# Projections of the next batch in another order over steps 9 to 15: logits ahead of k, the second group's q and k ahead of the V tiles, the ranks behind a V tile

## The chip, the cores and the metric

The kernel runs on one core of one Trainium2 chip. The metric is the device time of one execution in microseconds (us); lower is better. The engines are TensorE (PE; its weight loads are shown apart as PEld), VectorE (DVE), ScalarE (ACT), GpSimd (POOL) and SyncE (SP), whose queue starts most of the transfers.

## The reference

A layer over 8 batches of 512 tokens with 512 features: a layer norm, then attention with 16 heads and position bias, then a gate from a feed-forward block with two experts, of which each token uses the one with the larger logit.

```python
xn = layernorm(x)
qkv = xn @ Wqkv.T + b_qkv                       # 16 heads of 32
scores = q @ k.T * scale + alibi; causal mask
s = softmax(scores) @ v @ Wout.T + b_out
logits = xn @ w_router.T                         # 2 experts
top_idx = argmax(softmax(logits)); top_weight = its probability
h = xn @ w_fc[e].T; a = square(h if h >= 0 else h / 2)
g = silu(top_weight * (a @ w_proj[e].T))         # e = top_idx
out = x + s * g
```

## The kernel before

The program is written out by hand for each engine, without a scheduler; engines meet at counting semaphores (`wait(engine, semaphore, value)`). It has two stages, attention with the projections and the routing of the tokens, and behind it the feed-forward block, which works on tokens sorted by expert. The change touches the first.

Attention goes through the batches b = -1 to 8, each in 16 **steps**, one for each head. Iteration -1 is the start-up: it holds only the projections for batch 0. In a step TensorE turns the head's softmax weights (`ptrans`, line 446, in three parts into the banks psT0, psT1 and psT2), and computes the scores of the head four steps ahead (`scores`, line 425: four row groups of 128, 256, 384 and 512 columns in psS0, psS1 and psS2). Around and between them it does **jobs**. The list `JOBS` names each as (kind, batch relative to b, index), and `STEP` says which entries of the list belong to which step. The kinds are:

- `x`: turn 128 normalised tokens of the next batch (line 409).
- `q`, `k`: project one group of four heads, twelve matmuls of 512 columns (line 352, weights `wqkv` against `xT`). ScalarE copies the result out of PSUM (line 519), VectorE makes its high half (the **cast**, line 782), GpSimd its low half (line 947). SP's queue stores both to memory (line 280) and loads them back in the layout of the scores (line 285, function `stack`). Group 0 is read first by the scores of step 12 of the iteration before its own.
- `v`: the V tile of 128 tokens, twelve matmuls too; ScalarE copies it (line 544).
- `logits`: the router's logits, 48 matmuls of 2 columns; VectorE evaluates them (`choose`, lines 788 to 800).
- `rank`: two small matmuls (lines 400, 401) that count the tokens of each expert. VectorE turns them into positions (**place**, lines 807 to 823); GpSimd scatters the tokens' records with them in steps 14 and 15 (line 969).
- `ctx`: softmax weights times V of four heads (line 461), always the last work of its step. ScalarE copies it (line 528) at the beginning of the next step.
- `o`: the output projection.

Jobs use two PSUM banks in turn, psA0 and psA1: entry p of the list has the bank p mod 2, and `bank` lets it wait for the reader of the entry before in the same bank. So the order of `JOBS` sets the waits too. The other engines go through a step in a fixed order: VectorE takes a reciprocal for a head, masks and reduces the four score groups of the head three steps ahead (line 857), then does the reading for this step's jobs, then copies psT2 (line 844), and in some steps reduces a piece of the expert weights (line 888). GpSimd normalises the next head (line 941, four instructions), then makes q's or k's low half, and at steps 2, 7, 11 and 15 the context's (line 961). ScalarE copies psT0 and psT1 (line 566) and does the exponentials (line 579).

```python
            for p in STEP[step]:
                kind, db, i = JOBS[p]
                if job_exists(b, p) and kind in kinds:
                    yield kind, b + db, i, (odd + db) % 2, psA[p % ABANKS]
```

Of the kernel before, what the change touches and what calls it, by code (L numbers as in the profile page):

```python
# [95 lines left out]
def batches(eng, iteration):  # L96

    for b in range(-1, B + 1):
# [4 lines left out]
JOBS = [("q", 0, 2), ("ctx", -1, 3), ("k", 0, 2), ("q", 0, 3), ("k", 0, 3),  # L103
# [5 lines left out]
STEP = [(0, 1), (2,), (3,), (4,), (5, 6, 7), (8, 9), (10, 11), (12, 13),  # L109
        (14, 15), (16,), (17, 18), (19,), (20, 21), (22, 23), (24,), (25,)]  # L110
WMAX_AT = (5, 8, 12, 14)
WMAX_LAST = (2, 4, 9, 11)
ROUTE_AT = (1, 3, 5, 6)
# [1328 lines left out]
```

## Time and profile before

| what | value |
|---|---|
| median of 3 runs | 1499.54 us (1494.94 to 1501.87) |
| the profiled execution, whole | 1497.08 us |
| its span in the trace | 1495.3 us |
| mean granted TensorE clock | 0.984 of full |
| TensorE busy (matmuls) | 1392.0 us, 93% |
| VectorE busy | 929.4 us, 62% |
| ScalarE busy | 770.8 us, 52% |
| GpSimd busy | 684.8 us, 46% |

The attention stage fills a little more than the first half of the span, about 87 to 88 us for each batch. A busy share is a mean over stages; a busy TensorE is not one at its peak, since weights are loaded and instructions issued within it. The span leaves out what lies around it, here 1.8 us. In a row of the timeline stand the start, the length, the engine, the line, the operation and what is written and read; brackets give how long the engine was idle before, and who ended that.

### The profile page before, as it was taken

What the parts mean: (1) busy time and instruction counts of PE and PEld (TensorE: products, weight loads), DVE (VectorE), ACT (ScalarE), POOL (GpSimd) and SP (SyncE); (2) the same over time, 40 slices, a digit from 0 to 9 for tenths busy, and PEclk for the clock granted to TensorE, in tenths of its full rate; (3) what the DMA queues carried; (4) which work ended last, traced back from release to release, by engine and by line L of the source; (5) the groups of instructions that cost most, each with busy time, mean ns of one, the idle gap of its engine ahead of it and who ended that gap; (6) DMA issues with size and microseconds to landing.
All of it is one profiled execution on the core that took longest, in us unless ns stands there. A gap on an engine that the chain in (4) does not pass through costs nothing.

```text
span 1495.3 us, 30039 instructions
## 1 busy us (share of the span) xinstructions
PE 1392.0 (93%) x9863; PEld 883.6 (59%) x9863; DVE 929.4 (62%) x2441; ACT 770.8 (52%) x1824; POOL 684.8 (46%) x896
## 2 busy tenths in 40 slices
PE   2889999999999999999879999999999999999995
PEld 1455555655556565555546666666666666666663
DVE  7577776777767767777759855554445555544443
ACT  3477777777777777777736522222222222222221
POOL 0365656565575746556623433333333333333332
PEclk9999999999999999999999999999999999999998
DMA  4424424343342434334347411100111111001100
GB/s 159 142 85 133 136 93 142 113 129 107 117 146 92 149 99 136 107 111 148 106 141 229 139 44 44 43 29 24 35 43 41 39 43 44 24 27 38 36 29 29
DMA packets 84897, 133.45 MB, mean 89 GB/s; under 512 B 14095, under 2 KB 63247, under 8 KB 82576
## 3 DMA queue, kind: packets, MB, share of 16 engines
q1 hardware_dynamic: 75808, 105.70, 22.4%
q0 software_dynamic: 8944, 25.83, 5.5%
q8 instruction: 89, 1.46, 0.4%
q14 instruction: 56, 0.46, 0.1%
HBM read 97.81 MB, written 33.95 MB: 88 GB/s over the span
## 4 chain that ended last, share of the span: by engine, by line
PE 74%; DVE 11%; POOL 6%; issue 3%; ACT 3%; DMA 1%; DVEq 1%; SPq 0%; ACTq 0%; POOLq 0%
PE psF L1106 20%; PE psY L1126 19%; PE psA L352 18%; PE psT L446 7%; PE psA L461 5%; POOL pr L941 4%; PE psS L425 3%; DVE sg L1303 2%; PE psX L1080 1%; POOL route L969 1%; ACT stage L519 1%; PE psA L409 1%; DVE pr L857 1%; DVE stat L749 1%; DVE am L636 1%
## 5 line engine op out<-in xcount | busy, mean ns | idle before, releaser
L1106 PE MATMUL psF<-xT,wf 128*128 128x256 f16 (+1 forms) x3264 | 368.0, 269 | 0.0
L1126 PE MATMUL psY<-wf,aT 128*128 x1584 | 363.9, 379 | 0.4 <-DVE aT L1270 0.4
L1106 PEld LDWEIGHTS psF<-xT,wf 128*128 x3264 | 312.0, 98 | 63.5
L1344 POOL TENSOR_TENSOR a<-a 128x512 f32<-128x512 f32 (+1 forms) x136 | 153.3, 1127 | 391.0 <-DVE a L1261 389.4
L941 POOL TENSOR_SCALAR pr<-pr,rden 128x128 f32<-128x128 f32 (+3 forms) x512 | 269.7, 547 | 134.8 <-DVE rden L868 133.3
L579 ACT ACTIVATE pr<-pr,mn 128x128 f32<-128x128 f32 (+3 forms) x512 | 281.9, 553 | 0.0
L857 DVE CUSTOM_DVE_ANT_0 pr<-psS,base,nsl 128x128 f32<-128x128 f32 (+3 forms) x512 | 249.9, 543 | 2.4 <-PE psS L425 2.4
L1126 PEld LDWEIGHTS psY<-wf,aT 128*128 128x128 f16 x1584 | 154.5, 98 | 158.5 <-issue 1.1
L446 PE MATMUL psT<-conf,pr 128*128 128x128 f32 x1280 | 208.5, 282 | 21.2 <-POOL pr L941 17.2
L1183 ACT ACTIVATE rl<-psF 128x512 f32<-128x512 f32 (+1 forms) x136 | 79.3, 583 | 263.5 <-PE psF L1106 262.9
L446 PEld LDWEIGHTS psT<-conf,pr 128*128 128x128 f32 x1280 | 159.1, 144 | 87.3 <-POOL pr L941 27.1
L352 PE MATMUL psA<-xT,wqkv 128*128 128x512 f16 x768 | 195.2, 393 | 15.4 <-DVE wqkv L667 14.1
L1190 ACT ACTIVATE aT<-a 128x512 f16<-128x512 f32 (+1 forms) x136 | 84.0, 618 | 229.5 <-POOL a L1344 229.5
L1261 DVE SCALAR_TENSOR_TENSOR a<-psF,rl 128x512 f32<-128x512 f32 (+1 forms) x136 | 91.7, 674 | 169.3 <-ACT rl L1183 168.5
L566 ACT ACTIVATE pt<-psT 128x512 f32<-128x512 f32 x256 | 151.7, 593 | 80.6 <-PE psT L446 77.4
L1270 DVE TENSOR_TENSOR aT<-a,aT 128x512 f16<-128x512 f32 (+1 forms) x136 | 91.4, 672 | 129.0 <-ACT aT L1190 116.0
L352 PEld LDWEIGHTS psA<-xT,wqkv 128*128 128x128 f16 x768 | 76.7, 101 | 86.6 <-DVE wqkv L667 13.5
L947 POOL TENSOR_TENSOR pre<-stage,pre 128x512 f16<-128x512 f32 x64 | 74.3, 1161 | 110.1 <-DVE pre L782 110.1
L425 PE MATMUL psS<-ks,qs 128*128 128x128 f16 (+3 forms) x512 | 100.8, 304 | 22.7 <-DVE mn L857 18.9
L782 DVE CAST pre<-stage 128x512 f16<-128x512 f32 x64 | 33.7, 527 | 124.6 <-ACT stage L519 124.5
L352 PE MATMUL psA<-wout,cx 128*128 128x512 f16 x384 | 93.5, 386 | 7.3 <-POOL cx L961 7.3
L579 ACT ACTIVATION_READ_ACCUMULATOR pr<-pr,mn 128x1 f32 x512 | 98.3, 192 | 0.0
(155 smaller groups left out, 1371.5 us busy)
## 6 DMA issues: line engine op xcount, KB each, us to landing
qk_parts<-pre SPq DMA_DIRECT2D x64, 256.0 KB, 2.2
qs<-qk_parts SPq DMA_DIRECT2D x128, 128.0 KB, 2.7
ks<-qk_parts SPq DMA_DIRECT2D x128, 128.0 KB, 2.7
wst<-in_wf SPq DMA_DIRECT2D x16, 1024.0 KB
wstage<-in_wf SPq DMA_DIRECT2D x32, 512.0 KB, 5.0
xin<-in_x SPq DMA_DIRECT2D x32, 256.0 KB
attn_out<-so SPq DMA_DIRECT2D x32, 256.0 KB, 2.0
pt<-in_wqkv SPq DMA_DIRECT2D x4, 768.0 KB, 10.3
```

The lines of the kernel that those rows point to most:

```text
L352: last = nc.tensor.matmul(ps, a, x, start=(n == 0), stop=(n == len(pairs) - 1))
L425: nc.tensor.matmul(rows[i], qs[:, par, j, i * P:(i + 1) * P], ks[:, par, j, 0:(i + 1) * P], start=True, stop=True).then_inc(s["S_done"], 1)
L446: last = nc.tensor.transpose(ps[:, o:o + P], pr[:, j, c:c + P], conf[:, C_ID:C_ID + P])
L566: nc.scalar.activation(pt[:, g % 2, j, o:o + w], psT[r][:, 0:w], ACT.Copy).then_inc(s["T_act"], 1)
L579: nc.scalar.activation(p_, p_, ACT.Exp, bias=mn[:, c:c + 1], scale=-1.0, accum_out=den[:, c:c + 1]).then_inc(s["exp_done"], 1)
L857: nc.vector.tensor_tensor_reduce(out=pr[:, h % HG, ROWOFF[i]:ROWOFF[i] + w], in0=rows[i], in1=base[:, S - w:S], scale=nsl[:, h:h + 1], sca ...
L941: nc.gpsimd.tensor_scalar(p_, p_, rden[:, c:c + 1], 32768.0, ALU.mult, ALU.mult).then_inc(s["norm_done"], 1)
L1106: last = nc.tensor.matmul(psF[c % 2][:, k * TT:k * TT + tn], w(e, 2 * hc, hl, kc * 512 + col, P), xT[:, r % 2, x, kc, 0:tn], start=(m == 0 ...
L1126: last = nc.tensor.matmul(psY[r % 2][h][:], aT[:, c % 4, x, k, h * P:(h + 1) * P], w(e, 2 * hc + 1, hl, q * 512, 512), start=(c == 0 and k ...
L1261: nc.vector.scalar_tensor_tensor(out=part(a[:, c % 2, :], n), in0=part(psF[c % 2][:], n), scalar=2.0 ** -28, in1=part(rl[:, c % 2, :], n), ...
L1270: tt(aT[:, c % 4, 1, :, 0:tn], part(a[:, c % 2, :], n), aT[:, c % 4, 0, :, 0:tn], ALU.subtract).then_inc(s["U_lo"], 1)
L1344: nc.gpsimd.tensor_tensor(at, at, at, ALU.mult).then_inc(s["a_ready"], 1)
```

## The change

Two tables change, no function. The instructions stay the same in number and kind; their order over steps 9 to 13 and their banks change. In step 9 the logits come ahead of k of group 0, in steps 10 and 11 stand q and k of group 1, and V's four tiles follow in steps 12 to 15. In step 13 the V tile comes first and the rank behind it, though their places in the list are the other way round (`(23, 22)`), so V has psA1 and the rank psA0.

```diff
-        ("q", 1, 0), ("ctx", 0, 1), ("k", 1, 0), ("logits", 1, 0), ("v", 1, 0),
+        ("q", 1, 0), ("ctx", 0, 1), ("logits", 1, 0), ("k", 1, 0), ("q", 1, 1),
...
-        (14, 15), (16,), (17, 18), (19,), (20, 21), (22, 23), (24,), (25,)]
+        (14, 15), (16, 17), (18,), (19,), (20, 21), (23, 22), (24,), (25,)]
```

By steps this is:

| step | before | after |
|---|---|---|
| 8 | q0, ctx1 | q0, ctx1 |
| 9 | k0 | logits, k0 |
| 10 | logits, v0 | q1 |
| 11 | v1 | k1 |
| 12 | q1, ctx2 | v0, ctx2 |
| 13 | k1, rank | v1, rank |
| 14, 15 | v2; v3 | v2; v3 |

The first place is TensorE in step 13 of a middle batch, from the end of the context on. In brackets stands what an instruction waits for; `qk_staged` and `ctx_staged` are ScalarE's copies of a projection and of the context, `V_out` that of V. Before:

```order
L461 MATMUL psA1<-pt,v 32x128 x4
L446 MATMUL psT0<-conf,pr 128x128 [waits T_act,norm_done]
L446 MATMUL psT0<-conf,pr 128x128 x3
L352 MATMUL psA0<-xT,wqkv 128x512 [waits qk_staged]
L352 MATMUL psA0<-xT,wqkv 128x512 x5
L446 MATMUL psT1<-conf,pr 128x128 [waits T_act]
L446 MATMUL psT1<-conf,pr 128x128 x3
L352 MATMUL psA0<-xT,wqkv 128x512 x6
L400 MATMUL psA1<-e16,lt16 128x5 [waits e_ready,ctx_staged]
L401 MATMUL psA1<-epre,ones16 128x5
```

After, at the same place:

```order
L461 MATMUL psA1<-pt,v 32x128 x4
L446 MATMUL psT0<-conf,pr 128x128 [waits T_act,norm_done]
L446 MATMUL psT0<-conf,pr 128x128 x3
L352 MATMUL psA1<-wqkv,xT 128x512 [waits ctx_staged]
L352 MATMUL psA1<-wqkv,xT 128x512 x5
L446 MATMUL psT1<-conf,pr 128x128 [waits T_act]
L446 MATMUL psT1<-conf,pr 128x128 x3
L352 MATMUL psA1<-wqkv,xT 128x512 x6
L400 MATMUL psA0<-e16,lt16 128x5 [waits e_ready,V_out]
L401 MATMUL psA0<-epre,ones16 128x5
```

The wait for the context's copy has moved from the rank to the first matmul of the step's projection, which is now V's.

The second place is VectorE in step 13, from the last masked score group to the beginning of place (`rk` are the ranks, `R2_done` their matmuls). Before:

```order
L857 ISA pr,mn<-psS2,base,nsl 128x512 [waits S_done]
L857 ISA mn 128x1
L782 CAST pre<-stage 128x512 [waits k_stored,qk_staged]
L807 TENSOR_SCALAR rk<-psA1,esum 128x5 [waits meta_out,rexp_done,R2_done]
L810 COPY esum<-rk 128x1 [waits rank_read]
```

After:

```order
L857 ISA pr,mn<-psS2,base,nsl 128x512 [waits S_done]
L857 ISA mn 128x1
L807 TENSOR_SCALAR rk<-psA0,esum 128x5 [waits meta_out,rexp_done,R2_done]
L810 COPY esum<-rk 128x1 [waits rank_read]
L811 TENSOR_TENSOR t0<-tid,rk 128x4
```

The cast of k's second group, with its wait for ScalarE, has left the place ahead of the ranks; it stands in step 11 now.

The third place is TensorE in step 9 of a middle batch, behind the turning into psT0 (`wr` are the router's weights). Before, the twelve matmuls of k stood there alone. After:

```order
L446 MATMUL psT0<-conf,pr 128x128 x3
L352 MATMUL psA0<-wr,xT 128x2 [waits qk_staged]
L352 MATMUL psA0<-wr,xT 128x2 x41
L446 MATMUL psT1<-conf,pr 128x128 [waits T_act]
L446 MATMUL psT1<-conf,pr 128x128 x3
L352 MATMUL psA0<-wr,xT 128x2 x6
L352 MATMUL psA1<-xT,wqkv 128x512 [waits ctx_staged]
```

The logits' matmuls come from step 10; k follows them and has changed its bank. The order of SP's queue is the same, since it takes q and k group by group in either version.

## Rows read from the trace of the kernel before

**Rows 1.** The page's head and TensorE's row: busy time, share, instructions.

```profile
span 1495.3 us, 30039 instructions
...
PE 1392.0 (93%) x9863; PEld 883.6 (59%) x9863; DVE 929.4 (62%) x2441; ACT 770.8 (52%) x1824; POOL 684.8 (46%) x896
```

**Rows 2.** Waits over the whole span: total us, times, longest us.

```profile
PE psT L446 <- POOL pr L941: 17.2, 18, 1.9
```

**Rows 3.** Waits of TensorE from 403.3 to 410 us, same columns.

```profile
PE psS L425 <- DVE mn L857: 0.8, 3, 0.3
PE psT L446 <- DVE pt L844: 0.3, 1, 0.3
```

**Rows 4.** Timeline of TensorE, steps 12 to 0 of batch 3: start, length, line.

```profile
399.51 1.46 PE L352 MATMUL psA<-xT,wqkv 128*128 128x512 f16 x6
...
402.56 0.17 PE L401 MATMUL psA<-epre,ones 128*128 128x5 f16 x1
...
409.27 0.39 PE L425 MATMUL psS<-ks,qs 128*128 128x512 f16 x1 [0.33 <-DVE mn L857]
...
414.22 0.66 PE L446 MATMUL psT<-conf,pr 128*128 128x128 f32 x4 [0.20 <-POOL pr L941]
```

**Rows 5.** Timeline of ScalarE, step 13 of batch 3.

```profile
399.15 0.78 ACT L528 ACTIVATE cf<-psA,bqs,sc 128x512 f32<-128x512 f32 x1 [1.50 <-PE psA L461]
...
402.74 0.78 ACT L519 ACTIVATE stage<-psA,bqs,sc 128x512 f32<-128x512 f32 x1
```

**Rows 6.** Timeline of VectorE, steps 13 and 14 of batch 3.

```profile
403.55 0.43 DVE L782 CAST pre<-stage 128x512 f16<-128x512 f32 x1 [2.46 <-ACT stage L519]
...
403.89 0.22 DVE L807 TENSOR_SCALAR rk<-psA,esum 128x5 f32<-128x5 f32 x1
...
406.85 0.42 DVE L844 COPY pt<-psT 128x256 f32<-128x256 f32 x1
...
408.46 0.74 DVE L857 CUSTOM_DVE_ANT_0 pr<-psS,base,nsl 128x512 f32<-128x512 f32 x1
```

**Rows 7.** Timeline of TensorE: first instruction of steps 9, 10, 11.

```profile
378.43 0.66 PE L446 MATMUL psT<-conf,pr 128*128 128x128 f32 x4
...
382.72 0.60 PE L446 MATMUL psT<-conf,pr 128*128 128x128 f32 x4
...
388.18 0.60 PE L446 MATMUL psT<-conf,pr 128*128 128x128 f32 x4
```

**Rows 8.** Timeline of VectorE, steps 9 and 10 of batch 3.

```profile
382.97 0.43 DVE L782 CAST pre<-stage 128x512 f16<-128x512 f32 x1 [2.47 <-ACT stage L519]
...
385.68 0.22 DVE L788 TENSOR_SCALAR lg<-psA,sc 128x8 f32<-128x8 f32 x1
...
387.70 0.06 DVE L800 MEMSET t<- 128x1 f32 x1
```

**Rows 9.** Timeline of GpSimd, batch 3, behind step 9.

```profile
384.62 2.08 POOL L941 TENSOR_SCALAR pr<-pr,rden 128x128 f32<-128x128 f32 x4
```

**Rows 10.** Timeline of SP's DMA queue, batch 3: k's store behind step 9.

```profile
386.95 0.38 SPq L280 DMA_DIRECT2D qk_parts<-pre  x1
```

**Rows 11.** Timeline of the start-up: TensorE, ScalarE, VectorE.

```profile
58.16 0.17 PE L401 MATMUL psA<-epre,ones 128*128 128x5 f16 x1
...
59.26 2.75 PE L352 MATMUL psA<-wqkv,xT 128*128 128x512 f16 x12 [0.37 <-ACT stage L519]
...
58.33 0.78 ACT L519 ACTIVATE stage<-psA,bqs,sc 128x512 f32<-128x512 f32 x1 [7.40 <-PE psA L352]
...
59.48 0.22 DVE L807 TENSOR_SCALAR rk<-psA,esum 128x5 f32<-128x5 f32 x1
```

**Rows 12.** Waits of TensorE from 53 to 65 us, in the start-up.

```profile
PE psS L425 <- DVE mn L857: 1.8, 3, 1.2
```

**Rows 13.** Windows of two batches: length, busy by engine, mean clock, DMA.

```profile
168.35:255.12 86.77, 82.72 (x610) 49.22 (x610) 64.49 (x226) 66.48 (x181) 52.91 (x83) 1.00 0.39 123
255.12:343.60 88.48, 84.37 (x611) 50.09 (x611) 64.51 (x226) 66.48 (x181) 52.91 (x83) 0.98 0.39 120
```

2 rows, old and new, of the table JOBS are left out of this document.

## The prediction

> **What bounds the kernel now.** I read the page's head first. TensorE's matmul row is busy for 1392.0 of 1495.3 us [rows 1], so a microsecond is gained only where TensorE waits, and lost only where it is made to wait. The waits view says on whom: besides the start-up it waits on ScalarE, VectorE and GpSimd in short pieces, the longest of them 1.9 us, for GpSimd's normalisation of a head [rows 2]. The change touches steps 9 to 15 of a batch, so I laid the timelines of all engines over each other for one batch of the middle (b = 3, steps 9 to 15 from 378.4 to 418.6 us). From step 9 to the end of step 13 TensorE has no wait there at all. The waits stand behind it: in 403.3 to 410 us it waits 0.8 us for the row maxima and 0.3 us for a turned tile, both VectorE's [rows 3]. The same pieces stand at the same place in each of the seven batches b = 0 to 6, within 0.02 us. In the last batch there are no projections.
>
> What is late there can be followed back on VectorE [rows 6]. In step 13 the split of k's second group (the cast) starts at 403.55 us, since it waits for ScalarE's copy of k out of PSUM, 402.74 + 0.78 us [rows 5]. Only behind it comes the placing of the tokens (place): it starts at 403.89 and ends with the copy of psT2 at 406.85. Yet its own input, the rank, left TensorE at 402.56 + 0.17 = 402.73 us [rows 4]. So place, about 3 us of small dependent instructions, stands 1.1 us in a queue behind a cast that it doesn't need. All that follows on VectorE is late by it: the last masked row group at 408.46, and by it TensorE's last score matmul at 409.27 [rows 4, 6]. From there the lateness is carried on: GpSimd starts its normalisation late, sends its two scatters and normalises again, and TensorE's next step 0 starts at 414.22 with another 0.20 us of waiting for it [rows 4].
>
> **The change part by part.** The same instructions run, so all cost or gain is in waits.
>
> *Step 13, place first.* With k's second group in step 11, no cast stands before place. It can start when the rank is there. The first V product of step 13 pays for that: it now goes into the bank that the context of step 12 has just left, so it waits for ScalarE's copy of that context. This copy starts at 399.15 and takes 0.78, until 399.93 [rows 5]. How long TensorE takes to go on after such a copy is seen in the start-up: copy 58.33 + 0.78 = 59.11, matmul at 59.26, so 0.15 us [rows 11]. V would start at 400.08; the projection in its place starts at 399.51 now [rows 4]. That is a new wait of 0.57 us. The rank leaves 0.57 later, at 403.30; VectorE takes some 0.1 us to see it (my estimate, of the size of the 0.15 above), and place starts at 403.40 in place of 403.89: 0.49 us earlier. Because TensorE waits for VectorE in step 14 anyway, the 0.57 doesn't add to the end. By VectorE the last score matmul can come at 409.27 - 0.49 = 408.78. By its own work TensorE would have been there at 409.27 - 1.15 = 408.12 (1.15 is the sum of its waits, [rows 3] rounded), and now is there at 408.69. The later of the two holds: 408.78, with 0.1 us of waiting left of the 1.15. GpSimd's chain to 414.22 starts from the same VectorE instructions, so it moves by the same 0.49. Seven batches: 7 x 0.49 = 3.4 us. What queues behind the new wait is V's twelve matmuls, a transposition, the rank and the next scores, all of which have VectorE as their reader.
>
> The copy's length is worth a second look. The Trainium skill ("VectorE: DVE Perf Modes", section on the TRN2 errata) gives ScalarE reading PSUM 172 cycles plus one per element, at 1.2 GHz: (172 + 512) / 1.2 = 570 ns. The row has 0.78 us, with a bias and a scale from memory. By the page V would wait 0.21 us less and the sum would be 1.5 us larger; the measurement decides, and I stay with 0.78.
>
> *Start-up (b = -1).* The same queue, without a context ahead of V. The rank leaves at 58.16 + 0.17 = 58.33, place starts at 59.48 behind the cast [rows 11]. With 0.1 us to see it: 58.43, so 1.05 us earlier. TensorE then waits 1.8 us in three score matmuls for VectorE [rows 12], so the 1.05 goes through. The 0.37 us that V waits at 59.26 for k's copy goes too, but lies inside the same 1.05. Before that, k's first group comes behind the logits and its cast behind their evaluation; the scores wait for k's way through memory. That way goes through SP's queue, where q's loads stand ahead of k's store. I cost this at nothing, since in the start-up, too, the queue is what k's store waits for; the other bound is the evaluation's 2.0 us [rows 8], once, were the store to be late by all of it.
>
> *Steps 9 and 10, logits ahead of k.* The logits make step 10 last 388.18 - 382.72 = 5.46 us against 382.72 - 378.43 = 4.29 of step 9 [rows 7]. These 1.17 us move one step ahead; the sum of both is the same. On VectorE the evaluation takes 385.68 to 387.70 [rows 8]. In step 9 it can start once the logits are there, about 380.6 us by my estimate (378.43, two rounds of four transpositions and the 1.17), and ends near 382.6; k's cast, at 382.97 + 1.17 = 384.14 us [rows 8], waits for the copy of k anyway: evaluation costs nothing as long as VectorE idles there (it idles 2.47 us before that cast); without this cover it would be 2.0 us. k's store on SP's queue is at 386.95 behind q's loads [rows 10]. GpSimd ends k's low half at 384.62 in the trace [rows 9] and 1.17 later, at 385.79, in the new order, so the store stays where it is, and so do the scores that read it in step 12.
>
> *Steps 10 to 12, q and k of the second group, then V.* Each of these steps keeps its twelve matmuls of 512 columns. What is new is that three steps in a row (9, 10, 11) hand GpSimd a low half ahead of the next head's normalisation. In the trace the normalisation behind k's low half runs 384.62 to 386.70 [rows 9]. In the new order it ends 1.17 later, at 387.87; TensorE asks for it at 388.18 [rows 7]. The cover is 0.3 us. Cost nothing, bounds nothing and 0.2 us for each of three steps (4.2 us in seven batches). The stores and loads of this group move some 7 us ahead on SP's queue; in front of them stand k's loads of the first group, which they don't pass, and behind them x and the weights, which come earlier.
>
> *Sum.* -3.4 - 1.05 = -4.5 us. The profiled execution took 1497.08 us; it becomes 1492.6. The runs' median is 1499.54, 2.5 us above that execution, so I predict **1495.0 us**.
>
> **The rivals.** *The wait of V is hidden, or the clock falls less often.* If V finds its bank free, place starts 1.06 us earlier in each batch: 7 x 1.06 + 1.05 = 8.5 us, 1491.0. Against it speaks that the copy can't start before the context's last matmul. A batch in which TensorE's clock falls is 88.48 us at a mean of 0.98, one without is 86.77 at 1.00 [rows 13]: 1.71 us for each fall. Moving waits can take away two falls or add two (3.4 us either way). Chance of this rival 20%.
>
> *Nothing comes of it.* Place is earlier but GpSimd's row of normalisations in steps 10 to 12 passes its cover of 0.3 us: at 0.2 us beyond it, in three steps and seven batches, 4.2 us are given back. Time 1499 us. The thin margin speaks for it; against it, that the cover was worked out from rows that repeat to 0.02 us. Chance 17%.
>
> *Slower: the clock.* V's new wait of 0.57 us in step 13 and the 0.1 left in step 14 might bring TensorE from 2.4 to 1.2 GHz for a stretch in each batch. At 1.71 us a fall that is 12.0 us in seven batches, 7.5 slower in all: 1507 us. It decides from three falls on (5.1 against 4.5). Against it: step 14 waits 1.1 us today, more than the 0.7 us of both, and a batch that holds this wait still has a mean clock of 1.00 [rows 3, 13]; the fall in the other follows the long wait, up to 1.9 us, which the change leaves. Chance 8%. The Trainium skill ("TensorE: Matmul & The Clock Gate", section "What's actually happening") has the clock go down after an idle stretch and up after a busy one; by it alone no fall would be due, and 1495.0 would stand. The trace has falls after waits with matmuls between them, so the rule is no full cover.
>
> **How the numbers follow.** The forecast (3 to 6 us gained) has 55%, the rivals 20, 17 and 8%. A measurement of this kernel tells a change from none at about 0.5%, 7.5 us: the three runs of before lie 7 us apart. The first rival is faster than that; with some of the forecast's upper edge I give 25% to faster. The last rival is the 8% of slower, the rest, 67%, is the same. The range goes from the first rival with two falls fewer (1491.0 - 3.4, rounded to 1487.5) to no gain with one or two falls more (1499.5 + 2.5 = 1502); it leaves out the last rival and some of the edges.
>
> **What would show it.** Right: in the middle batches the place instructions start behind the masked rows with VectorE idle before them, waiting for TensorE's rank; a wait of 0.4 to 0.7 us of TensorE on ScalarE's context copy at the start of step 13, seven times; the score waits of step 14 shorter, about 0.1 in place of 1.15 us; a batch without a fall 86.3 us. Wrong: TensorE waits on GpSimd in steps 10 to 12; place still begins behind something else; more stretches at 1.2 GHz than before.

## The result: 1.3% faster, outside the predicted range

| | before | after |
|---|---|---|
| median | 1500.70 us (4 runs, 1494.94 to 1502.18) | 1480.60 us (4 runs, 1477.33 to 1481.51) |
| profiled execution; its span | 1497.08; 1495.3 us | 1481.51; 1479.7 us |
| mean granted TensorE clock | 0.984 | 0.987 |

The ratio is 0.9874 (95% interval 0.9857 to 0.9891): 20.1 us less by the medians, 15.6 us by the two profiled executions, where 4.5 were forecast. The timeline of TensorE in the same batch as [rows 4, 7], steps 10 to 0:

```profile
377.08 0.60 PE L446 MATMUL psT<-conf,pr 128*128 128x128 f32 x4
...
392.36 0.66 PE L446 MATMUL psT<-conf,pr 128*128 128x128 f32 x4
393.32 1.47 PE L352 MATMUL psA<-wqkv,xT 128*128 128x512 f16 x6 [0.31 <-ACT cf L528]
...
396.39 0.17 PE L401 MATMUL psA<-epre,ones 128*128 128x5 f16 x1
...
397.21 0.60 PE L446 MATMUL psT<-conf,pr 128*128 128x128 f32 x4
...
399.38 1.46 PE L352 MATMUL psA<-wqkv,xT 128*128 128x512 f16 x6
400.68 0.38 PE L446 MATMUL psT<-conf,pr 128*128 128x128 f32 x2
400.89 0.71 PE L425 MATMUL psS<-ks,qs 128*128 128x128 f16 x4
401.44 0.63 PE L446 MATMUL psT<-conf,pr 128*128 128x128 f32 x4
...
406.04 0.66 PE L446 MATMUL psT<-conf,pr 128*128 128x128 f32 x4 [0.19 <-POOL pr L941]
```

The step starts stand at 392.36 (13), 397.21 (14) and 401.44 (15). Step 14 now holds no wait at all. VectorE in steps 13 and 14, to be laid beside [rows 6]:

```profile
396.61 0.23 DVE L807 TENSOR_SCALAR rk<-psA,esum 128x5 f32<-128x5 f32 x1 [3.14 <-PE psA L401]
...
396.94 0.15 DVE L811 TENSOR_TENSOR t<-tid,rk 128x4 f32<-128x4 f32 x1
...
398.71 0.42 DVE L844 COPY pt<-psT 128x256 f32<-128x256 f32 x1
...
400.31 0.75 DVE L857 CUSTOM_DVE_ANT_0 pr<-psS,base,nsl 128x512 f32<-128x512 f32 x1
```

Place begins behind 3.14 us of idle time, 0.05 after the rank's end (396.39 + 0.17), and takes 2.10 us to the copy of psT2; it took 2.96 in [rows 6]. The 0.86 between them is one instruction. These are rows of the kernel before that the prediction had not looked at, from the timelines of VectorE, GpSimd and TensorE:

```profile
404.21 1.02 DVE L811 TENSOR_TENSOR t<-tid,rk 128x4 f32<-128x4 f32 x1
...
404.06 1.16 POOL L947 TENSOR_TENSOR pre<-stage,pre 128x512 f16<-128x512 f32 x1 [2.72 <-DVE pre L782]
...
399.02 0.65 PE L446 MATMUL psT<-conf,pr 128*128 128x128 f32 x4
...
403.38 0.60 PE L446 MATMUL psT<-conf,pr 128*128 128x128 f32 x4
...
405.55 1.46 PE L352 MATMUL psA<-wqkv,xT 128*128 128x512 f16 x6
407.33 0.44 PE L446 MATMUL psT<-conf,pr 128*128 128x128 f32 x2 [0.32 <-DVE pt L844]
408.06 0.34 PE L425 MATMUL psS<-ks,qs 128*128 128x128 f16 x2 [0.30 <-DVE mn L857]
408.60 0.34 PE L425 MATMUL psS<-ks,qs 128*128 128x384 f16 x1 [0.20 <-DVE mn L857]
...
409.57 0.66 PE L446 MATMUL psT<-conf,pr 128*128 128x128 f32 x4
```

L811, the third instruction of place, subtracts two operands of four columns in SBUF. It ended at 404.21 + 1.02 = 405.23, and GpSimd's low half of k, which started 0.15 us ahead of it and ran beside it, at 404.06 + 1.16 = 405.22. All eight instances in the trace of before take 1019 to 1027 ns, all eight after 150 to 153 ns, with no low half beside them. Step lengths of TensorE, from such starts, in us:

| step | 9 | 10 | 11 | 12 | 13 | 14 | 15 | sum |
|---|---|---|---|---|---|---|---|---|
| before | 4.29 | 5.46 | 4.23 | 6.61 | 4.36 | 6.19 | 4.65 | 35.79 |
| after | 5.52 | 4.23 | 4.22 | 6.83 | 4.85 | 4.23 | 4.61 | 34.49 |

The logits' 1.2 us moved from step 10 to 9 at no cost. Step 12 is 0.22 longer: VectorE's high half of the context (L900), 0.42 us in most instances, takes 1.28 there, again beside GpSimd's low half of k, which now falls on it. The seven kernels of this study with such a cast of 1.27 to 1.28 us have a step 12 of 6.81 to 6.83 us, the other five one of 6.61; no run takes the collision away alone, so this cause is argued and not shown.

```profile
386.29 1.16 POOL L947 TENSOR_TENSOR pre<-stage,pre 128x512 f16<-128x512 f32 x1 [1.04 <-DVE pre L782]
...
386.46 1.28 DVE L900 CAST cx<-cf 128x512 f16<-128x512 f32 x1
```

Steps 13 and 14 together fell from 10.55 to 9.08 us, by 1.47. The whole batch, in the windows view (columns as in [rows 13]):

```profile
391.56:477.02 85.46, 82.21 (x614) 49.27 (x610) 63.95 (x226) 66.44 (x181) 52.70 (x82) 1.00 0.41 127
```

It is 85.46 us against 86.77 without a fall of the clock. Between the first and the last full batch's place, before needs 527.49 us for six batches, four of them with a fall (88.46), after 512.80 without any: 6 x 1.31 + 4 x 1.71 = 14.7 us. That is nearly the whole 15.6; the part ahead of it is level and the part behind it gives 0.9.

### The profile page after: what moved, and what is told of

The parts are those of the page before. It is cut to its first block, busy times and chain, and to the rows that moved or that the text cites. A ratio compares the mean times of both kernels' runs of the same rounds, so it can differ in the third digit from the quotient of the medians.

```text
span 1479.7 us, 30039 instructions
## 1 busy us (share of the span) xinstructions
PE 1384.0 (94%) x9863; PEld 880.8 (60%) x9863; DVE 923.9 (62%) x2441; ACT 770.7 (52%) x1824; POOL 682.5 (46%) x896
## 4 chain that ended last, share of the span: by engine, by line
PE 75%; DVE 10%; POOL 6%; ACT 3%; issue 3%; DMA 1%; DVEq 1%; SPq 0%; ACTq 0%; POOLq 0%
PE psY L1126 19%; PE psF L1106 19%; PE psA L352 19%; PE psT L446 7%; PE psA L461 5%; POOL pr L941 4%; PE psS L425 3%; DVE sg L1303 2%; PE psX L1080 1%; POOL route L969 1%; PE psA L409 1%; DVE stat L749 1%; DVE am L636 1%; ACT stage L519 1%; DVE wf L1225 1%
## 5 line engine op out<-in xcount | busy, mean ns | idle before, releaser
L352 PE MATMUL psA<-xT,wqkv 128*128 128x512 f16 x768 | 188.8, 386 | 14.4 <-DVE wqkv L667 13.1
```

The costliest lines, as they stand in the source:

```text
L352: last = nc.tensor.matmul(ps, a, x, start=(n == 0), stop=(n == len(pairs) - 1))
```

## The experiments

The medians are of 4 to 11 executions each, on chips on which the kernel before had medians of 1499.88 (first four), 1499.73 (next four) and 1501.02 us (last two). The ratio is that to the kernel before on the same chip; the whole change has 0.9874, so variants whose intervals overlap with 0.9857 to 0.9891 aren't told apart from it by their time. "Falls" counts those of TensorE's clock in the six batches just named, in the one execution of each that has a trace.

| run | median us | ratio (95%) | batch without a fall | falls in 6 |
|---|---|---|---|---|
| rank_first | 1480.23 | 0.9869 (0.9851 to 0.9887) | 84.65 | 2 |
| low_late | 1500.51 | 1.0006 (0.9997 to 1.0015) | 86.65 | 4 |
| lock_back | 1494.21 | 0.9961 (0.9948 to 0.9975) | 86.42 | 3 |
| logits_first | 1500.27 | 1.0004 (0.9995 to 1.0013) | 86.80 | 5 |
| pad3 | 1488.37 | 0.9927 (0.9911 to 0.9943) | 86.12 | 2 |
| pad6 | 1498.45 | 0.9991 (0.9981 to 1.0001) | 86.76 | 5 |
| v_bank | 1478.04 | 0.9850 (0.9834 to 0.9866) | 84.98 | 2 |
| rank_first_after | 1478.28 | 0.9856 (0.9838 to 0.9874) | 84.50 | 3 |
| rstd_late | 1496.57 | 0.9973 (0.9963 to 0.9983) | 86.93 | 5 |
| rstd_late_vbank | 1480.04 | 0.9866 (0.9851 to 0.9881) | 85.17 | 0 |

**Only step 13 (rank_first).** The kernel before, with the rank ahead of k's product; the transpositions into psT1, which stand between the halves of a product, move ahead of the rank (`mid()`).

```diff
-        (14, 15), (16,), (17, 18), (19,), (20, 21), (22, 23), (24,), (25,)]
+        (14, 15), (16,), (17, 18), (19,), (20, 21), (23, 22), (24,), (25,)]
...
                 ps = bank(b, p)
+                mid()
                 wait(pe, s["e_ready"], batch + 1)
```

> The kernel before with one pair of numbers changed: in step 13 the rank comes ahead of k's second group (with psT1's transpositions ahead of both), nothing else is moved. Theory 1 (step 13 alone: place stands behind the cast, and its first two-operand instruction, 1.02 us in the trace of before against 0.15 after, is held by GpSimd's low half beside it): place starts right behind the masked rows, is over before the cast, L811 takes 0.15 us, step 14 falls from 6.19 to about 4.23 us, a batch without a fall of the clock from 86.77 to about 84.8, so at least 13 us less than before (7 x 1.9), more if falls of the clock go away. Theory 2 (the gain comes from moving q and k ahead of V in steps 10 to 12): no gain beyond the 0.6 us that I had worked out for place, under 5 us.

Measured: 1480.23 us, as good as the whole change. Its timeline of VectorE (lines one higher):

```profile
390.65 0.22 DVE L808 TENSOR_SCALAR rk<-psA,esum 128x5 f32<-128x5 f32 x1
...
390.98 0.15 DVE L812 TENSOR_TENSOR t<-tid,rk 128x4 f32<-128x4 f32 x1
...
393.30 0.43 DVE L783 CAST pre<-stage 128x512 f16<-128x512 f32 x1 [0.47 <-ACT stage L520]
```

Place stands ahead of the cast, so ahead of the low half that follows it, and its L812 is short. Steps 13 and 14 last 4.39 and 4.22 us. A batch is 0.81 us shorter than in after: V has no new wait (0.48), step 12 no collision (0.22), and step 15 is 0.16 shorter. So everything that the change gains in a batch can be had from the order of place and cast; moving V, q, k and the logits isn't needed for it.

**Only the low half away (low_late).** The kernel before; in step 13 GpSimd makes k's low half only when place has ended.

```diff
                     w = int(kind == "k")
+                    if step == 13:
+                        wait(pool, s["meta_ready"], nxt + 1, s["apart_pool"])
```

> The kernel before, but GpSimd makes k's low half of step 13 only when place is over; the order of the jobs stays, and place stays behind the cast. Theory 1 (GpSimd's low half holds VectorE's two-operand instruction): L811 falls from 1.02 to 0.15 us, place is 0.87 us shorter, step 14 falls from 6.19 to about 5.3 us, 6 us less in seven batches. Rival (L811 is long for a reason of its own, as waiting for its input): L811 stays at 1.02 us and the time as before.

Measured: no change, where 6 us had been expected. L811 fell to 0.15 us although place still stood behind the cast, so the low half was what held it. But the low half now stands in front of the normalisation on GpSimd's queue, and TensorE waits for that instead at the start of step 15; step 14 is 6.07 us, not the 5.3 expected:

```profile
405.97 1.16 POOL L949 TENSOR_TENSOR pre<-stage,pre 128x512 f16<-128x512 f32 x1 [4.89 <-DVE rk L823]
407.11 2.05 POOL L941 TENSOR_SCALAR pr<-pr,rden 128x128 f32<-128x128 f32 x4
...
409.22 0.66 PE L446 MATMUL psT<-conf,pr 128*128 128x128 f32 x4 [0.67 <-POOL pr L941]
```

**The neighbour put back (lock_back).** The kernel after, with an added GpSimd subtraction of the low half's size on two constant tiles, released by the rank. Its result is not used.

```diff
+                if more and step == 13:
+                    wait(pool, s["R2_done"], nxt + 1, s["apart_pool"])
+                    nc.gpsimd.tensor_tensor(scrap[:], bout[:], base[:], ALU.subtract)
```

> The changed kernel with one extra GpSimd instruction per batch in step 13: a subtraction of 128x512 between two constant tiles into a scratch tile, started when the rank is there, so beside place. Theory 1: L811 is about 1.0 us again in place of 0.15; the last masked rows come 0.87 us later, of which TensorE feels about 0.75 after a slack of 0.1, so 5 us more than the changed kernel in seven batches, about 1486 us, if the clock falls as it does there. Rival (L811's length has nothing to do with GpSimd): 0.15 us and 1480.6.

Measured: 1494.21 us, 13.6 of the 20 us given back, where 5 had been expected.

```profile
403.83 1.01 DVE L812 TENSOR_TENSOR t<-tid,rk 128x4 f32<-128x4 f32 x1
...
403.55 1.27 POOL L952 TENSOR_TENSOR scrap<-bout,base 128x512 f16<-128x512 f32 x1 [2.95 <-PE psA L402]
```

The two end together again (404.84 and 404.82), though no semaphore ties them and no tile is common. A batch is 0.96 us longer; steps 13 and 14 are 4.85 + 5.08 = 9.93 us. This splits the 1.47: from 10.55 to 9.93 the earlier start of place, 0.62; from 9.93 to 9.08 the end of this collision, 0.85. The rest of the 13.6 is falls: 7 x 0.96 = 6.7, and four falls more (three in the six batches, one behind them), 6.8.

**Only the logits (logits_first).** The kernel before with the logits ahead of k, and nothing else.

```diff
-        ("q", 1, 0), ("ctx", 0, 1), ("k", 1, 0), ("logits", 1, 0), ("v", 1, 0),
+        ("q", 1, 0), ("ctx", 0, 1), ("logits", 1, 0), ("k", 1, 0), ("v", 1, 0),
...
-        (14, 15), (16,), (17, 18), (19,), (20, 21), (22, 23), (24,), (25,)]
+        (14, 15), (16, 17), (18,), (19,), (20, 21), (22, 23), (24,), (25,)]
```

> The kernel before with the first part of the change alone: logits ahead of k in step 9, the V tile alone in step 10; steps 11 to 15 as before. Theory 1: no effect, 1500 us within 3, steps 9 and 10 only exchange 1.2 us. Theory 2 (part of the gain comes from here, as the evaluation of the logits leaves step 10, where GpSimd normalises beside it): some us less, L792 falls from 0.51 to 0.16 us, and a batch is shorter by some tenths.

Measured: no change, 86.80 us a batch. In the start-up it isn't free: the first scores start at 54.15 us, in before at 53.32. k's store goes out 0.26 us later, and its loads 3.4 us behind the store and not 2.9. Why the loads come later isn't shown; in the traces with the logits first they follow the store by anything from 2.2 to 3.8 us.

**The same work, longer (pad3, pad6).** The kernel after, with 3 or 6 further matmuls of 512 columns in each batch, ahead of the logits, whose results are overwritten. They ask whether the missing falls hang on the order or on the batch's length. Here with 6:

```diff
                 ps = bank(b, p)
+                for t in range(6):
+                    nc.tensor.matmul(ps[:], wqkv[:, 0, 0, 0:P], xT[:, par, 0, 0, :], start=True, stop=True)
```

> As the kernel with six more matmuls per batch, but three: 0.65 us more per batch, 86.1 us. Theory 1: 1480.6 + 4.5 and some falls of the clock (1 to 4), 1487 to 1492 us. Rival (no falls by length): 1485.1 us.

> The changed kernel with six more matmuls of 512 columns per batch ahead of the logits (their results are overwritten), 6 x 0.216 = 1.3 us of TensorE work, which makes a batch as long as it was before the change: 86.8 us. Theory 1 (the falls of TensorE's clock behind the wait of step 3 come with how the batches lie in time, not with the order of the jobs): 3 to 5 falls in batches 1 to 6 where the changed kernel's trace has none, time 1480.6 + 9.1 + 4 x 1.7 = 1496.5 us. Rival (the change took the falls away itself, with step 14's waits): no falls there, 1480.6 + 9.1 = 1489.7 us.

Measured: 1.30 us more in each batch (pad6) is 9.1 us, and the time rose by 17.9; 0.66 (pad3) is 4.6, and it rose by 7.8. The difference is 8.8 and 3.2 us, and 5 and 2 falls at 1.71 are 8.6 and 3.4. Two windows of pad6, a batch with a fall and one without:

```profile
404.64:493.07 88.43, 85.15 (x618) 50.70 (x616) 63.96 (x227) 66.55 (x182) 52.72 (x82) 0.98 0.38 119
493.07:579.83 86.76, 83.51 (x618) 49.89 (x616) 63.94 (x226) 66.53 (x182) 52.72 (x82) 1.00 0.39 122
```

With the new order and the old length the falls are back, as the theory of both runs had it. So the new order of jobs doesn't by itself keep them away.

**V's wait (v_bank, rank_first_after).** The kernel after; v_bank exchanges V and rank in the list and keeps V first, so V no longer waits for the context's copy. rank_first_after puts the rank first, as in rank_first.

```diff
-        ("k", 1, 1), ("v", 1, 0), ("ctx", 0, 2), ("rank", 1, 0), ("v", 1, 1),
+        ("k", 1, 1), ("v", 1, 0), ("ctx", 0, 2), ("v", 1, 1), ("rank", 1, 0),
...
-        (14, 15), (16, 17), (18,), (19,), (20, 21), (23, 22), (24,), (25,)]
+        (14, 15), (16, 17), (18,), (19,), (20, 21), (22, 23), (24,), (25,)]
```

> The changed kernel with the V tile and the rank of step 13 exchanged in the list of jobs, so that they change banks; their order in the step stays. V no longer waits for ScalarE's copy of the context. Theory 1: the wait of 0.31 us (0.47 from start to start) at the head of step 13 goes, a batch 85.0 us in place of 85.46, 3.3 us less in seven batches if the clock falls as in the changed kernel. Rival (VectorE bounds step 14 again, as place isn't earlier by the same): no gain.

> The changed kernel with the rank ahead of the V tile in step 13, behind the transpositions into psT1. Theory 1: place starts behind the masked rows, V's wait for the context's copy is hidden by the transpositions; a batch 84.9 us against 85.46, 4 us less in seven batches. Against the kernel of before with the rank first (84.65 us) it is 0.2 us longer per batch, since the context's high half in step 11 meets GpSimd's low half of k (L900, 1.28 us) and step 12 is longer by 0.2. Rival (moving q and k has a gain of its own): shorter than 84.65 us.

Measured: step 13 is 4.37 us in v_bank, 0.48 less than in after, step 14 stays 4.22. The wait was in full on TensorE's path: 7 x 0.48 = 3.4 us, and two falls take the same back: the profiled spans are 1478.7 and 1479.7 us. The medians, 1478.04 and 1478.28, are the lowest of the study; their ranges overlap with that of after.

rank_first_after had been expected at 84.9 us a batch and is at 84.50, 0.15 under rank_first. There its rival held, that moving q and k has a gain of its own. Step 12 is 0.21 longer than in rank_first, but step 15 is 4.23 us against 4.45, with no wait for GpSimd at its end. By the timelines this takes both parts: no low half stands ahead of GpSimd's normalisation, as one does in rank_first, and place is over early, as it isn't in after (4.61). In time the two aren't told apart (1480.23 and 1478.28 us).

**The long wait moved (rstd_late, rstd_late_vbank).** GpSimd's inverse deviations of the layer norm (L953, L956) move from step 1 to step 2, behind the normalisation, and their use on VectorE from steps 2 to 5 to steps 3 to 6; once in before and once in v_bank.

```diff
-                    elif step < 6:
-                        ln_apply(step - 2)
+                    elif 3 <= step < 7:
+                        ln_apply(step - 3)
...
-                if more and step == 1:
+                if more and step == 2:
```

> The kernel before, with GpSimd's inverse deviations of the layer norm (veps and rstd, in step 1, ahead of the normalisation) moved to step 2 behind the normalisation, and the layer norm's application moved from steps 2 to 5 to steps 3 to 6. TensorE's wait for that normalisation is 1.80 us, and the inverse deviations wait 0.79 us for VectorE and take about 1.4 with what lies between. Theory (the falls of the clock hang on this wait): the wait shrinks to some 0.4 us, a batch is about 1.4 us shorter (85.3 without a fall) and no batch of 1 to 6 has a fall: 1499.7 - 9.8 - 6.8 = about 1483. Rival (falls come whatever the wait, as the batches lie in time): still 2 to 5 falls, about 1490. Rival on the other side: rstd now ends some 3 us later than today, the lows behind it too, and VectorE or SP's transfers wait for them: no shorter batch, about 1500.

> The same move of the inverse deviations and of the layer norm's application, on top of the changed kernel with V and rank exchanged in the list (1478.0 us, 2 falls in the middle batches, 84.98 us a batch). Theory: 83.6 us a batch without a fall and no fall: 1478.0 - 9.8 - 3.4 = about 1465, faster than both kernels. Rival: falls stay, about 1468. Other side: later lows are waited for, about 1478.

Measured: the move didn't do what it was made for. The wait of 1.80 us is only passed on, as one of 1.9, since GpSimd works without a pause through step 2 and the next normalisation ends late. So neither the shorter batch came (some 1483 and 1465 us had been expected), nor was the theory tested that the falls go when this wait goes. From rstd_late, GpSimd and TensorE:

```profile
428.36 1.04 POOL L950 TENSOR_TENSOR rstd<-veps,half 128x4 f32<-128x4 f32 x1
429.39 1.15 POOL L956 TENSOR_TENSOR pre<-stage,pre 128x512 f16<-128x512 f32 x1
430.51 1.15 POOL L961 TENSOR_TENSOR cx<-cf,cx 128x512 f16<-128x512 f32 x1
431.76 2.55 POOL L941 TENSOR_SCALAR pr<-pr,rden 128x128 f32<-128x128 f32 x4
...
434.36 0.66 PE L446 MATMUL psT<-conf,pr 128*128 128x128 f32 x4 [1.92 <-POOL pr L941]
```

A batch is 0.16 us longer than in before, and 0.19 longer than in v_bank. The profiled execution is level with that of before (1497.15 and 1497.08); where the medians' 4.4 us come from isn't settled. With the same wait of 1.9 us one kernel has 5 falls in six batches and the other none, so the wait alone doesn't decide.

## Why the prediction was wrong

**The term that was mis-sized** is that of "Step 13, place first": 7 x 0.49 = 3.4 us. Steps 13 and 14 measured 7 x 1.47 = 10.3, of which step 12 gave 7 x 0.22 = 1.5 back; with 0.06 in the other steps a whole batch is 1.31 us shorter, 9.2 in seven. The direction and the first link of the mechanism, place behind a cast that it doesn't need, were right. Three things made the term too small.

*Place's length.* The prediction carried "place, about 3 us of small dependent instructions" along at its old length. Inside stood L811 with 1.02 us beside neighbours of its kind at 0.16. low_late and lock_back show that GpSimd's low half was its cause, and lock_back what it costs: 0.85 us a batch, more than the whole forecast of 0.49. A look at each row of place, and at what GpSimd did in that microsecond, would have found it.

*The ceiling.* "By its own work TensorE would have been there at 409.27 - 1.15" summed the idle times in brackets. With it, no more than 1.15 us could have come out of step 14; 1.96 did (6.19 to 4.23). The matmuls' ends are modelled and overlap the next one's start: without a stall the turning of a tile starts 1.30 us behind the group of six matmuls ahead of it (399.38 to 400.68), with one 1.78 (405.55 to 407.33). That is 0.48 us lost where the bracket says 0.32. From the turning to the next step it is 0.76 without and 2.24 with waits, 1.48 lost, of which the brackets name 0.83. V's wait shows the same: 0.47 by the starts (393.32 - 392.36, against 0.49 without), 0.31 in brackets.

*The start of place.* It is 0.62 us earlier, not 0.49: V's wait is 0.47 and not 0.57, since TensorE goes on 0.05 us behind the copy (392.49 + 0.78, then 393.32) and not 0.15, and VectorE sees the rank after 0.05 and not 0.1. But "the 0.57 doesn't add to the end" held only under the lower gain. With the collision gone step 14 has no wait left to hide it, and v_bank shows its 0.48 in full.

**Steps 10 to 12** were costed at nothing, with GpSimd's cover of 0.3 us as the risk. The cover held: no wait of TensorE there. The cost came from elsewhere: 0.22 us in step 12, by all signs from the same kind of collision.

**Steps 9 and 10** at nothing: right. **Start-up** 1.05: by the end of it after is ahead by 1.03 us (V's product of step 14 starts at 63.66, before at 64.69), but by two terms, not one: the first scores start 1.04 late, which the prediction had put at nothing with 2.0 as bound, and the way from there on is 2.07 shorter (1.05 and the collision's 0.87 are 1.92 of it).

**The clock.** The prediction took falls as they were, with two more or fewer as a rival's edge. In the profiled executions four went away, 6.8 us; the two of the rival were a guess, no term of the sum led to four, and this part of the gain is luck. Its rival of 1491.0, "the clock falls less often", was nearer than the forecast, though V's wait was not hidden; "slower: the clock" was wrong, as the wait of 0.47 us brought no fall in any of seven batches. In the sum on the profiled basis, 4.5 forecast became 9.2 + 6.8 - 0.4 = 15.6; the 0.4 is what the start-up, the last batch and the falls in them leave together. The medians say 20.1; before's profiled execution lies 3.6 us under its median, the price of about two falls, though no trace shows that it is these.

**The rule behind the collision** is one that the prediction should have weighed. The Trainium skill ("SBUF — State Buffer", section "Who interferes with whom") says that a VectorE instruction with two SBUF inputs contends with a GpSimd instruction that reads SBUF, and that the second to come waits until the first has ended. The runs agree: 1.02 against 0.15 us for L811, which starts second in both kernels (by 0.15 us in before, by 0.28 in lock_back), and the ends 0.01 to 0.02 us apart. It also says that `cast` can take the shared ports when its operands meet certain conditions, which fits L900's 1.28 us against 0.42; no run here separates that.

## What to carry to other kernels

Before a block of instructions is moved as one length, read each of its rows: a small one that is far longer than its like may be waiting for a neighbour, as here, and then its length goes with the place. Take what a waiting engine could gain from the starts of a step with and without the wait, not from the sum of idle times. A short reordering of one pair (rank_first) was worth as much as the change of seven steps, so cut a change down to the pair that the trace names and time that first.

## What the hardware showed that was not expected

The falls of TensorE's clock (from 2.4 to 1.2 GHz for 3.4 us, 1.71 us lost) go with the length of a batch, but how many come at which length no theory here gives. Of six batches there fell, in order of the length without a fall: 84.50 us 3, 84.65 us 2, 84.98 us 2, 85.17 us 0, 85.46 us 0, 86.12 us 2, 86.42 us 3, 86.65 us 4, 86.77 us 4, 86.76 and 86.80 us 5 each, 86.93 us 5. All 35 of these falls begin near the end of the wait of 1.8 to 1.9 us for GpSimd, from 0.5 us ahead of it to 1.2 us behind it, but every batch has this wait, and all twelve batches of 85.17 and 85.46 us pass it at full clock. The place of the fall against the wait drifts from batch to batch: the four of before begin 0.13, 0.40, 0.69 and 0.94 us behind its end, and then one is left out. That suggests that it matters where in time the wait comes, which a batch's length shifts for all batches behind it; no run sets it on purpose. What decides it beyond that stays open; counts of falls also differ between executions of one kernel, as the spread of 7 us in before's runs suggests, and each kernel here has one trace. In a comparison of kernels with such a wait, 8.5 us in 1500 (five falls) can come from this alone.
